# Feed-forward: the score pairs of an item stand in other places on TensorE, seven of them ahead of the context; VectorE's transposition, reciprocal and maxima follow in the matching order

## What is computed

```python
def _mha(q, k, v, wq, wk, wv, wo):          # H = 8 heads of 16, S = 256 tokens of one of 8 batches
    qh, kh, vh = (q @ wq), (k @ wk), (v @ wv)          # each reshaped to (B, S, H, 16)
    scores = jnp.einsum('bqhd,bkhd->bhqk', qh, kh) / jnp.sqrt(dh)
    attn = jax.nn.softmax(scores, axis=-1)
    ctx = jnp.einsum('bhqk,bkhd->bqhd', attn, vh).reshape(B, S, d)
    return ctx @ wo
for c in range(6):                          # six nodes, each reads earlier nodes
    q = ew[c, 0] * (nodes[in_q] @ We[eq] + be[eq])     # k and v likewise
    nodes[c] = act_w[c] * _mha(q, k, v, Wq[c], Wk[c], Wv[c], Wo[c]) + q
return _layernorm(nodes[5], ln_g, ln_b)
...
x = x + 0.5 * _L0_ffn_ref(_layernorm(x), ...)
x = x + _L0_attn_ref(...)
x = x + 0.5 * _L0_ffn_ref(_layernorm(x), ...)
```

## Time and profile before

| | |
|---|---|
| median of 3 runs | 2154.4 us (2152.77 to 2157.96) |
| the profiled execution | 2160.08 us, its span 2157.8 us |
| granted TensorE clock, mean | 0.962 of full speed |
| span, busy: TensorE, VectorE, ScalarE, GpSimd | 91%, 80%, 60%, 54% |
| first feed-forward, 349 us of steady steps (79 to 428 us) | busy 338.71, 274.90, 223.60, 219.49 us, clock 1.00 |
| second feed-forward, 350 us of steady steps (880 to 1230 us) | busy 339.05, 275.74, 224.08, 219.68 us, clock 1.00 |

### The profile page before, as it was taken

One profiled execution on the slowest core, in us unless ns is written; L12 is line 12 of the kernel. 1 busy time (PEld: TensorE's weight loads), 2 busy tenths in 40 slices (PEclk: granted clock), 3 DMA queues, 4 the chain that ended last, 5 costly groups with the idle time before them and its releaser, 6 DMA issues. The chain is left out here.

```text
span 2157.8 us, 39266 instructions
## 1 busy us (share of the span) xinstructions
PE 1972.7 (91%) x14044; PEld 1440.9 (67%) x14044; DVE 1732.0 (80%) x2918; ACT 1293.5 (60%) x2495; POOL 1171.1 (54%) x1605
## 2 busy tenths in 40 slices
PE   6999999976999995999999968699999999999878
PEld 4566666644888873666666645577877877877746
DVE  5777777766888875777777766499999999999984
ACT  1566666643777773666666643567576685685633
POOL 3666666613776764666666612345736647556423
PEclk9899999997999996999999998899999999999989
DMA  4666565620000003556565505000000000000000
GB/s 133 146 156 151 150 155 150 151 84 1 1 2 2 2 2 78 143 155 149 151 156 150 149 21 201 0 1 1 1 1 1 1 1 1 1 1 0 1 15 20
DMA packets 147745, 144.85 MB, mean 67 GB/s; under 512 B 14049, under 2 KB 106977, under 8 KB 146913
## 3 DMA queue, kind: packets, MB, share of 16 engines
q1 hardware_dynamic: 127968, 132.91, 22.7%
q10 hardware_dynamic: 19584, 9.44, 2.4%
HBM read 94.07 MB, written 38.80 MB: 62 GB/s over the span
## 5 line engine op out<-in xcount | busy, mean ns | idle before, releaser
L573 DVE TENSOR_REDUCE sb_f_mx<-ps_f_s 128x2 f32<-128x512 f32 x768 | 494.6, 674 | 161.8 <-PE ps_f_s L354 160.4
L508 ACT ACTIVATE sb_f_pt<-ps_f_t 128x1024 f32<-128x1024 f32 x384 | 381.2, 1023 | 166.9 <-PE ps_f_t L371 109.0
L1935 POOL TENSOR_TENSOR sb_mb_h<-sb_mb_h 128x512 f32<-128x512 f32 x128 | 165.1, 1311 | 304.6 <-DVE sb_mb_h L1818 303.5
L354 PE MATMUL ps_f_s<-sb_f_stack 96*128 96x256 bf16 x1536 | 287.3, 280 | 42.7 <-DVE sb_f_mx L573 23.5
L1813 DVE TENSOR_TENSOR_SCAN sb_mb_h<-sb_mb_da,sb_mb_h 128x1024 f32<-128x1024 f32 x128 | 304.4, 2417 | 2.7 <-ACT sb_mb_da L1673 2.7
L1484 PE MATMUL ps_mb_f<-sb_mb_fc,sb_mb_cw 128*128 128x256 f32 x1280 | 285.1, 379 | 6.2 <-ACT sb_mb_fc L1686 6.1
L1484 PEld LDWEIGHTS ps_mb_f<-sb_mb_fc,sb_mb_cw 128*128 128x128 f32 x1280 | 238.5, 189 | 40.5 <-ACT sb_mb_fc L1686 8.4
L371 PE MATMUL ps_f_t<-sb_f_stack 128*128 128x256 bf16 x1536 | 235.7, 276 | 10.8 <-ACT sb_f_pt L508 6.0
L354 PEld LDWEIGHTS ps_f_s<-sb_f_stack 96*128 96x128 bf16 x1536 | 136.6, 99 | 151.1 <-issue 84.0
L1673 ACT ACTIVATE sb_mb_da<-sb_mb_dl,sb_mb_an 128x255 f32<-128x255 f32 x512 | 211.0, 496 | 31.3 <-DVE sb_mb_h L1813 30.7
L428 PE MATMUL ps_f_a<-sb_f_pt,sb_f_v 128*32 128x256 f32 x3072 | 188.3, 386 | 0.8 <-ACT sb_f_v L546 0.8
(11 more groups left out here) (248 smaller groups left out, 4011.5 us busy)
## 6 DMA issues: line engine op xcount, KB each, us to landing
f_scr<-sb_f_parts SPq DMA_DIRECT2D x96, 384.0 KB, 2.7
sb_f_stack<-f_scr SPq DMA_DIRECT2D x192, 192.0 KB, 3.1
sb_f_stack<-f_scr SPq DMA_DIRECT2D x192, 128.0 KB, 3.2
sb_f_stack<-f_scr SPq DMA_DIRECT2D x192, 64.0 KB, 3.3
sb_f_stack<-sb_f_mrow ACTq DMA_DIRECT2D x96, 96.0 KB
sb_mb_cw<-in_cw SPq DMA_DIRECT2D x1, 5120.0 KB, 19.7
sb_prep_wn<-in_wn SPq DMA_DIRECT2D x6, 512.0 KB, 7.1
sb_m_w<-in_w SPq DMA_DIRECT2D x6, 256.0 KB, 2.9
```

The lines of the kernel that those rows point to most:

```text
L354: last = nc.tensor.matmul(s_bank[j % 2][:, h, :], stack[0:ROWS, a.n % STACKS, 0, g * GROUP + pair * 2 + h, half * P:(half + 1) * P], stack ...
L508: nc.scalar.activation(pt[:, e.two, g, half, :, :], t_bank[i % 2][:, :, :], ACT.Exp).then_inc(s["pt_sb"], 1)
L573: nc.vector.tensor_reduce(mx[:, a.two, half, head:head + 2], s_bank[j % 2][:, :, :], AX.X, ALU.max)\
L1935: nc.gpsimd.tensor_tensor(hb[:, c, 0:2, :], hb[:, c, 0:2, :], hb[:, c, 2:4, :], ALU.add).then_inc(s["half_sb"], 1)
```

## The change

On TensorE the parts of the turned scores and the pairs are spread otherwise over a step. The second part of the turned scores, `scores_t(e, 1)`, moves behind pair 2, and with it the queries come straight behind pair 1; the third part moves from behind pair 2 to behind pair 4; pair 5 moves ahead of `output` and pair 6 ahead of the context, which is now one call. On VectorE `by_token` moves from the end of the step to the start of the next one, where it serves the same item, and is cut in two: the reciprocal (`invert`) stands behind the maximum of pair 0. `by_dim` moves from behind pair 1 to behind pair 3 and the node's addition from behind pair 4 to behind pair 5. No instruction is added or removed, no buffer and no wait.

```diff
             def context(u, g):
...
-                if g == NG - 1:
-                    last.then_inc(s["ctx_ps"], 1)
+                last.then_inc(s["ctx_ps"], 1)
...
                     scores(a, 1)
-                if e:
-                    scores_t(e, 1)
                 if f and step >= EXP_LAG:
                     queries(f)
                 if a:
                     scores(a, 2)
                 if e:
-                    scores_t(e, 2)
+                    scores_t(e, 1)
                 if a:
                     scores(a, 3)
                 values(m, e, o)
                 if a:
                     scores(a, 4)
+                if e:
+                    scores_t(e, 2)
+                if a:
+                    scores(a, 5)
                 if o:
                     output(o)
                 if a:
-                    scores(a, 5)
+                    scores(a, 6)
                 if u:
-                    context(u, 0)
-                    context(u, 1)
+                    context(u)
                 if a:
-                    scores(a, 6)
                     scores(a, 7)
...
                 if ending(step, TAIL_LAG) is not None:
                     center(ending(step, TAIL_LAG))
+                if o:
+                    by_token(o)
                 for j in range(8):
                     if a:
                         row_max(a, j)
-                    if o and j == 1:
+                    if o and j == 0:
+                        invert(o)
+                    if o and j == 3:
                         by_dim(o)
-                    if o and j == 4:
+                    if o and j == 5:
                         dve.wait_ge(s["out_ps"], o.n + 1)
...
-                if u:
-                    by_token(u)
```

More of the change, by code:

```diff
@@ L413, in values, with context @@
                     last.then_inc(s["v_ps"], 1)
-            def context(u, g):
+            def context(u):
                 e, m = (Item(x) if x < ITEMS else None for x in (u.n + 1, u.n + 2))
-                if g == 0:
-                    pe.wait_ge(s["pt_sb"], u.n * 4 + 4)
-                    if e:
[L421 to L431, removed]
-                if g == NG - 1:
-                    last.then_inc(s["ctx_ps"], 1)
+                pe.wait_ge(s["pt_sb"], u.n * 4 + 4)
+                if e:
+                    pe.wait_ge(s["v_sb"], e.n + 1)
+                    if m:
+                        pe.wait_ge(s["mrow_sb"], m.n + 1)
+                elif u.n:
+                    pe.wait_ge(s["ct_sb"], u.n)
+                for g in range(NG):
+                    for half in range(2):
+                        for h in range(GROUP):
+                            last = nc.tensor.matmul(act_bank[h * SLOT:(h + 1) * SLOT, g * N:(g + 1) * N],
+                                                    v[:, u.two, half, h * NG + g, :],
+                                                    pt[:, u.two, g, half, h, :], start=half == 0, stop=half == 1,
+                                                    tile_position=(0, h * SLOT))
+                last.then_inc(s["ctx_ps"], 1)
             def output(o):
@@ L574, in row_max, with by_token, invert @@
                     .then_inc(s["mx_sb"], 1)
[L576 to L580, removed]
+            def by_token(o):
+                dve.wait_ge(s["ctx_ps"], o.n + 1)
+                if o.n:
+                    dve.wait_ge(s["cn_sb"], o.n)
                 nc.vector.transpose(ct[:, :, :, :].rearrange("p g j e -> p (g j e)"), act_bank[:, :]).then_inc(s["ct_sb"], 1)
-                dve.wait_ge(s["ct_sb"], u.n + 1)
+            def invert(o):
+                dve.wait_ge(s["ct_sb"], o.n + 1)
                 nc.vector.reciprocal(rsum[:, :, :], ct[:, :, :, SUMROW]).then_inc(s["rsum_sb"], 1)
@@ L637, in _ @@
             for step in steps:
-                a, u, o = ffn_item(step, SCORE_LAG), ffn_item(step, SUM_LAG), ffn_item(step, OUT_LAG)
+                a, o = ffn_item(step, SCORE_LAG), ffn_item(step, OUT_LAG)
                 if ending(step, TAIL_LAG) is not None:
                     center(ending(step, TAIL_LAG))
+                if o:
+                    by_token(o)
                 for j in range(8):
```

## The result

| | before | after |
|---|---|---|
| median of 5 runs each | 2154.4 us | 2118.1 us (2116.02 to 2120.98) |
| ratio, 95% interval | | 0.9827, 0.9811 to 0.9842 |
| the profiled execution | 2160.08 us | 2119.61 us, its span 2117.8 |
| undisturbed step | 8.48 us | 8.09 us |
| first to 42nd context, first and second feed-forward | 349.31, 348.92 | 335.54, 335.65 |

A forecast was written before the change was run, and what follows sets the result against it. TensorE's 8.48 us step, with one wait for maximum 6, was taken as the bound. 41 steps by 0.21 plus 1.4 for last steps give 10.0 a feed-forward, 20 in both: profiled 2140, median 2134, range 2120 to 2149.

The forecast's parts named there:

- The handover: VectorE's maxima 0 and 1, behind `by_token` and the reciprocal, make TensorE's pairs 2 and 3 wait 0.20 us a step together.
- TensorE goes on 0.16 after a maximum's end: Pair 0's start behind maximum 6 (257.70 to 257.86), applied to pairs 2 and 3, forecast at 4.36 and 5.13.
- the 0.20: Waiting of TensorE ahead of pairs 2 and 3 together, in us a step, making the step 8.27.
- The positions of VectorE: From the context's start: maximum 7 at 2.30, `by_token` 2.90, maximum 0 3.53, reciprocal 4.13, maximum 1 4.30 us.
- What makes the step shorter: Pair 6 ahead of the context ends its maximum under it, so pair 0 needs no wait; 0.38 us were lost there.
- a closed ring through TensorE: Step before without late rows: 8.48 us, 8.10 of TensorE issue and 0.38 of pair 0 waiting for maximum 6.
- The `mrow` rows: DMA issue to turned part 0: 4.16 us against 4.10; late steps stay 8 in 41, costing 0.03 to 0.04 a step.
- The last steps: Steps 47 to 49 lose 0.7 us, three later node cycles gain 2.1 (8.07 instead of 8.76); net 1.4 a feed-forward.
- The handover is free: Rival, 9%: transposition and reciprocal leave TensorE no wait; step 8.07, time 2118.
- The dearer handover: Rival, 12%: maximum 0 starts 0.74 or more behind `by_token`, Vector instructions full durations apart; step 8.38 to 8.50, time 2143 to 2154.
- The rows land later: Rival, 7%, slower: the `mrow` DMA sets the step, with landings from 4.57 us in every step; at 4.7, time 2162.
- Nothing moves: Rival, 8%: TensorE loses elsewhere, for instance at pair 1 or in weight loads, what pair 0 gains; 2150 to 2156.

The follow-up runs named there:

- the control: Changed kernel with the full eight-head `mrow` DMA and only the exponent's input scaled by a ten-thousandth, so values are not the reference's: 2119.33 us, 0.9827.
- the kernel with the pairs alone: Kernel before, with only pair 5 moved ahead of `output` and pair 6 ahead of the context: 2156.36 us, 1.000, step 8.477.
- the version in which no pair waits: Changed kernel with `values` straight behind pair 2, turned part 1 behind pair 3, and `by_dim` behind maximum 2: 2118.89 us, 0.982.

## Why the prediction was wrong

By its own sum, of profiled executions: forecast 2140; steady steps, 82 times 8.09 instead of 8.27, -14.8; more late rows, +4.8 (7.8 instead of 3.0); last steps, -8.8 (-6.1 and -5.5 instead of -1.4 twice); the first context of the first feed-forward comes 2 us earlier behind its first maximum (28.52 instead of 30.53, in the second 30.47 instead of 30.40), for which I have no cause; over the two feed-forwards of all twelve traces this stretch takes anything from 28.3 to 31.5, and 29.2 twice in the control, whose order of instructions is that of the changed kernel, so it may be no effect of the change at all. That makes 2119 against 2119.6 measured.

**The handover, mis-sized.** The step that failed is "TensorE goes on 0.16 after a maximum's end". I took it from pair 0 in the earlier trace rows and used it for pairs 2 and 3, whose waits are not the same. Pairs 0 and 4 begin with two waits, first for the stack and then for the maximum; pairs 2 and 3 have the one for the maximum:

```python
if j % 4 == 0:
    pe.wait_ge(s[f"stack{g}"], 16 * len(RUNS) * (a.n + 1))
if a.n * 8 + j >= 2:
    pe.wait_ge(s["mx_sb"], a.n * 8 + j - 1)
```

For pairs 0 and 4 the trace before has the wait for the maximum as an instruction of its own, 51 ns long: 190 times, which is both pairs of all 96 items but for the first pair of each feed-forward, which waits for no maximum (PEldq is the sequencer of the weight loads):

```profile
L350 PEldq EVENT_SEMAPHORE  x190: 51/51/51, 47.2 to 1254.2; - x190
```

At pair 0 it stands (257.76 to 257.81) between the end of maximum 6 and the weight load of the pair, which starts 0.12 after that end; the weight load of pair 2 in the changed kernel starts 0.05 after the end of maximum 0 (before, then after):

```profile
257.83 0.13 PEld L354 LDWEIGHTS ps_f_s<-sb_f_stack 96*128 96x128 bf16 x2 [0.47 <-issue]
```

```profile
250.18 0.14 PEld L354 LDWEIGHTS ps_f_s<-sb_f_stack 96*128 96x128 bf16 x2 [0.20 <-DVE sb_f_mx L572]
```

Where a pair is held up by a maximum, in all twelve traces, its first matmul starts 0.15 after the maximum's end if it is pair 0 or 4 (226 times) and 0.06 after it for every other pair (534 times). It makes no difference whether VectorE sat idle before that maximum or came straight from another instruction. No experiment took the wait for the stack away, so that the second wait is what costs the 0.09 rests on these rows.

The second part of the term is the maximum's own length: 0.69 out of idleness, as at pair 0, but 0.65 behind the transposition and 0.63 behind the reciprocal, where I had 0.67 for both. Between start and start, pair 0 thus costs 0.83 (257.03 to 257.86), pairs 2 and 3 0.68 to 0.71 where they are on the path: 243.25 to 243.94 and 252.15 to 252.83 in the experiments, and in the changed kernel, in the last steps of the first feed-forward, where pair 2 waited 0.73:

```profile
425.23 0.65 DVE L572 TENSOR_REDUCE sb_f_mx<-ps_f_s 128x2 f32<-128x512 f32 x1
```

```profile
425.93 0.39 PE L354 MATMUL ps_f_s<-sb_f_stack 96*128 96x256 bf16 x2 [0.73 <-DVE sb_f_mx L572]
```

With 0.65 + 0.06, pair 2 is due at 3.53 + 0.71 = 4.24 and TensorE is free at 4.27; with 0.63 + 0.06, pair 3 is due at 4.26 + 0.69 = 4.95, where it comes, 0.01 to 0.02 later than TensorE alone would. That is all that is left of the 0.20. What remains beside it is the 0.2 us that the weight load of pair 2 waits, which lies under the queries' matmuls.

**The positions of VectorE, right**: 0.63 behind `by_token`, and the rule of the Trainium skill that I set against it (VectorE: DVE Perf Modes, The DRAIN you can't avoid) would have asked for 0.71. The same section adds "A next op that is not held starts earlier", which I had left out, so the page did not speak against the 0.63 as flatly as the prediction has it. The rows show 0.63 (248.84 to 249.47), 0.58 from maximum 0 to the reciprocal, and 0.15 behind the reciprocal, where I had 0.60 and 0.17: maximum 1 starts at 4.26 and not at 4.30.

**What makes the step shorter, right in its place but half the story.** The wait for maximum 6 went, as said. I hadn't seen the ring through the exponent that lay on it; had the change not moved part 1 too, the gain would have been nothing, as the kernel with the pairs alone shows. The 8.48 of before were said to be "a closed ring through TensorE" with one loss of 0.38. They were two, and the wait for maximum 6 could be forecast away only because the diff opened both. The 0.03 by which TensorE's costs came out under 8.10 was not rounding, as I had it: 0.02 of it is part 1 waiting for the exponent, and the version in which no pair waits has a step of 8.07, the sum of the costs.

**The `mrow` rows, wrong in number.** The interval was as forecast: from the issue at 244.53 to part 0 at 248.69 it is 4.16 us, and 4.10 before. But the landing takes longer (in the median 2.95 instead of 2.3 to 2.5), and the issue stands closer behind the first load of the stack (2.76 us instead of 3.20). In the kernels that send all eight heads' rows the median landing grows as this distance shrinks, from 2.3 at 3.6 us to 3.5 at 2.0. That is all that links them: of the changed kernel's 13 landings that took 3.65 to 4.20 us, ten come in steps with the usual distance (2.5 to 2.9 us), and what singles these steps out is open. The late steps doubled and cost 7.8 us. The pairs' waits that I had counted on as a cushion do not exist.

**The last steps, right in kind, mis-sized.** The additions hide the context's wait, as said, and steps 48 and 49 lose 0.36 each, the 0.7 of the forecast. The sum over a cycle had "3.03 for the additions (468.03 to 471.06)" in it. Now, on VectorE:

```profile
447.98 0.48 DVE L654 TENSOR_SCALAR sb_f_node<-ps_f_d,sb_ffn_bo 128x256 f32<-128x256 f32 x1 [1.23 <-PE ps_f_d L442]
448.38 0.16 DVE L613 RECIPROCAL sb_f_rs<-sb_f_sd 128x2 f32<-128x2 f32 x1
448.57 0.61 DVE L618 SCALAR_TENSOR_TENSOR sb_x<-sb_f_ty,sb_f_rs,sb_x 128x128 f32<-128x128 f32 x2
...
451.03 0.46 DVE L598 BATCH_NORM_STATS2 sb_f_st<-ps_f_s 128x6 f32<-128x128 f32 x2
...
452.27 0.71 DVE L580 STREAM_TRANSPOSE sb_f_ct<-ps_f_a 128x512 f32<-128x512 f32 x1
...
455.67 0.48 DVE L654 TENSOR_SCALAR sb_f_node<-ps_f_d,sb_ffn_bo 128x256 f32<-128x256 f32 x1 [1.22 <-PE ps_f_d L442]
```

From node to node it is 7.69 instead of 8.07, and the whole difference lies between 448.38 and 451.03: 2.65. `center` (1.24) and all behind it are as in the sum. The pair of additions that was 1.05 long is 0.61. Before the change (VectorE, then GpSimd):

```profile
468.17 1.05 DVE L616 SCALAR_TENSOR_TENSOR sb_x<-sb_f_ty,sb_f_rs,sb_x 128x128 f32<-128x128 f32 x2
```

```profile
468.19 0.62 POOL L698 TENSOR_TENSOR sb_f_cn<-sb_f_ct,sb_f_rsum 128x256 f32<-128x256 f32 x1 [6.29 <-DVE sb_f_rsum L583]
```

The long pair runs beside GpSimd's product. Now the product comes behind `center` (at 453.34), beside nothing but the wait for it. All 32 additions (minimum, median, longest in ns), before, after, and with both turns of VectorE back at the end:

```profile
L616 DVE SCALAR_TENSOR_TENSOR sb_x<-sb_f_ty,sb_f_rs,sb_x x32: 339/349/786, 468.2 to 1298.2; 128x128 f32<-128x128 f32 x32
```

```profile
L618 DVE SCALAR_TENSOR_TENSOR sb_x<-sb_f_ty,sb_f_rs,sb_x x32: 343/348/353, 448.6 to 1257.8; 128x128 f32<-128x128 f32 x32
```

```profile
L618 DVE SCALAR_TENSOR_TENSOR sb_x<-sb_f_ty,sb_f_rs,sb_x x32: 338/348/786, 455.0 to 1272.9; 128x128 f32<-128x128 f32 x32
```

786 ns appear where the product falls on the additions, and not where only `by_token` is put back ahead of them (343/348/352). In all twelve traces, 30 additions have the product beside them and take 782 to 786 ns, and the 354 others at most 354 ns. The Trainium skill states it (GPSIMD Engine Reference, Specifications): GpSimd and VectorE share their interfaces to SBUF and collide when the Vector instruction has two inputs there, as this one has. The trace agrees, at 0.44 us a time for the addition, while the product takes 0.62 beside it as it does alone. The prediction took 3.03 over into an order in which the product no longer stands beside it. The following two cycles shrank by more (9.55 to 7.96, and 10.65 to 9.32 in the first feed-forward). Before, the second of their contexts ran in part at the lower clock (granted 0.50 of full speed, 1.2 GHz, at 482 to 484 us, a context of 2.82 us) and VectorE waited 2.31 for it; now the context of 3.35 us at the same clock (0.50 at 464 to 466) runs under the additions. And 2.1 us of the first feed-forward's 6.1 is one step: before, a stretch with a granted clock of 0.58 (430 to 434 us), at the same place 1.00 after. Whether the change has a part in that, nothing here shows.

**The rivals.** "The handover is free" had 9% and gave 2118, the time measured, and its mechanism is what happened; that the number fits so well is partly luck, since the dearer rows (+4.8) and the better last steps (-8.8) half cancel. "The dearer handover" is refuted by 0.63 and 0.70. "The rows land later" was half right: they do, but in single steps and for 4.8 us; the rival had them late in every step, at 8.61 a step and 2162. "Nothing moves" is refuted by the step of 8.09, but it is what the pairs alone would have given, through a wait that the prediction hadn't in view.

## What to carry to other kernels

When one wait is taken out of a ring, look for a second ring of the same length under it: take every buffer that is used again within the step, add up producer, consumer and handover from the starts, and compare, also where the trace shows no wait. Take a handover's price from a place that has the same waits in the program as the one to be forecast, and a duration from a stretch in which the engine's neighbours and the other engines do what they will do there. When the costs of a ring don't quite add up to it, look for what holds the difference before calling it rounding. A DMA moved to another place in the step has another landing time; its slack has to be counted against the transfers that it then falls in with.

## What the runs showed of the hardware that was not expected

- A pair of matmuls that waited for nothing but a maximum started 0.06 us after the maximum's end, and 0.15 after it where the program has the wait for the stack ahead of the one for the maximum.
- The same maximum (128 x 512 fp32) took 0.69 us out of idleness, 0.65 straight behind the transposition and 0.63 straight behind the reciprocal.
- An addition with two SBUF inputs (128 x 128 fp32) took 0.35 us alone and 0.79 with GpSimd's 0.62 us product beside it, which itself took no longer.
- The same 96 KB DMA of ScalarE's queue landed 2.3 to 2.5 us after its issue in the median when it was issued 3.2 us behind the first load of the stack, 2.95 at 2.76 us, 3.4 to 3.6 at 2.0 us, and with an eighth of the bytes after 2.1.
